# Fewer semaphore increments from TensorE, and scatters and gathers that no longer ask how far TensorE is

## The reference

```
agg = segment_sum(x[src], dst) / max(count, 1)                     # one matrix of edge counts serves all such sums
h   = relu(agg @ W1l.T + b1l + x @ W1r.T)                          # 256 -> 512
out = (segment_sum(h[src], dst) / count) @ W2l.T + b2l + h @ W2r.T # 512 -> 256
x   = layernorm(x + out)
# three hops:   H = segment_sum(H[src] * edge_weight, dst) @ Wn.T + H @ Ws.T + b   (elu between), x = layernorm(x + H)
# interaction:  messages (x @ W1)[src] + (x[src] * x[dst]) @ W2, scaled by degrees, summed by dst, then layernorm
# attention, 8 heads of 32, h = x @ W:
e   = leaky_relu(a_src[src] + a_dst[dst]);  m = segment_max(e, dst);  p = exp(e - m[dst])
out = segment_sum(h[src] * p, dst) / segment_sum(p, dst);  x = layernorm(x + layernorm(out + bias))
```

## Time and profile before

| | us |
|---|---|
| three runs | 2978.41, 2980.54, 2985.08 |
| median | 2980.54 |
| span of the profiled execution | 2974.2 |
| PE busy in the span | 2470.6 |
| DVE, ACT, POOL busy | 1396.0, 707.2, 936.7 |
| scatters L794 busy, 416 of them | 411.2 |
| gathers L2134 into `features_and_rows` busy, 376 of them | 401.7 |

### The profile page before, as it was taken

One profiled execution on the slowest core, in us unless ns is written; L12 is line 12 of the kernel. 1 busy time (PEld: TensorE's weight loads), 2 busy tenths in 40 slices (PEclk: granted clock), 3 DMA queues, 4 the chain that ended last, 5 costly groups with the idle time before them and its releaser, 6 DMA issues. The chain is left out here.

```text
span 2974.2 us, 32381 instructions
## 1 busy us (share of the span) xinstructions
PE 2470.6 (83%) x9483; PEld 1621.2 (55%) x9484; DVE 1396.0 (47%) x3940; ACT 707.2 (24%) x1552; POOL 936.7 (31%) x927
## 2 busy tenths in 40 slices
PE   3677789897987999999999999999977886457680
PEld 2444788343766555565556555577743444345560
DVE  7999656455665001030101001455575664546668
ACT  3776545111443000010001000255400000103112
POOL 0000256666666000000000000012167666576740
PEclk9888999998998999999999999999988998678885
DMA  6565678343344743444444434333558887646641
GB/s 233 243 253 225 212 238 264 118 138 97 112 121 137 152 151 129 151 134 151 129 152 133 151 119 145 93 106 102 113 168 271 278 282 245 209 132 190 192 127 43
DMA packets 209534, 493.89 MB, mean 166 GB/s; under 512 B 46457, under 2 KB 128430, under 8 KB 209134
## 3 DMA queue, kind: packets, MB, share of 16 engines
q1 hardware_dynamic: 135185, 301.30, 32.2%
q10 hardware_dynamic: 38173, 133.27, 12.8%
q0 software_dynamic: 36032, 57.60, 7.1%
HBM read 374.71 MB, written 117.32 MB: 165 GB/s over the span
## 5 line engine op out<-in xcount | busy, mean ns | idle before, releaser
L794 POOL DMA_INDIRECT table_dense_weights<-pair_weight,dst x416 | 411.2, 988 | 563.5 <-DVE weights_c L849 324.8
L1526 PE MATMUL banks<-own_term,features_and_rows 128*128 128x391 f32 (+1 forms) x1656 | 552.3, 491 | 0.0
L2134 POOL DMA_INDIRECT features_and_rows<-table_heads,src x376 | 401.7, 1068 | 191.4 <-issue 107.9
L1526 PEld LDWEIGHTS banks<-own_term,features_and_rows 128*128 128x128 f32 x1656 | 312.2, 189 | 226.8
L1552 DVE TENSOR_SCALAR features_and_rows<-banks,hop_bias 128x391 f32<-128x391 f32 (+1 forms) x24 | 15.0, 625 | 762.2 <-PE banks L1526 762.2
L954 PE MATMUL banks<-split_rows,count_columns 128*128 128x512 f32 x1200 | 322.1, 415 | 19.6 <-issue 12.6
L2531 PE MATMUL banks<-features_and_rows,edge_to_window 128*128 x880 | 233.4, 427 | 104.5 <-DVE edge_to_window L2492 71.6
L1526 PE MATMUL banks<-features_and_rows 128*128 128x391 f32 (+1 forms) x840 | 282.4, 491 | 0.0
L954 PEld LDWEIGHTS banks<-split_rows,count_columns 128*128 128x128 f32 x1200 | 226.3, 193 | 76.8 <-issue 21.7
L2531 PEld LDWEIGHTS banks<-features_and_rows,edge_to_window 128*128 128x128 f32 x880 | 181.3, 210 | 156.5 <-issue 122.5
L558 PE MATMUL banks<-features_and_rows,pair_and_bias_rows 128*128 128x400 f16 x806 | 184.3, 388 | 87.1 <-DVE features_and_rows L540 51.9
(11 more groups left out here) (425 smaller groups left out, 3016.8 us busy)
## 6 DMA issues: line engine op xcount, KB each, us to landing
hidden<-table_counts SPq DMA_DIRECT2D x305, 160.0 KB
table_dense_weights<-weights_c ACTq DMA_DIRECT2D x26, 1600.0 KB, 5.7
own_term<-table_dense_weights SPq DMA_DIRECT2D x52, 782.0 KB
features_and_rows<-table_rows_by_edge SPq DMA_DIRECT2D x58, 528.0 KB
own_term<-table_dense_weights SPq DMA_DIRECT2D x34, 780.5 KB
pair_and_bias_rows<-table_edge_rows ACTq DMA_DIRECT2D x50, 512.0 KB
weights_c<-table_edge_rows ACTq DMA_DIRECT2D x50, 512.0 KB
table_rows_by_edge<-features_and_rows SPq DMA_DIRECT2D x48, 528.0 KB
```

Source lines behind the costliest of these rows:

```text
L794: e.indirect_dma_start(out=self.table, out_offset=bass.IndirectOffsetOnAxis(ap=self.place[:, t:t + 1], axis=0), in_=self.values[:, t:t + 1 ...
L1526: m = e.matmul(psum[b][:, 0:wide], z_block(block)[:, f * P:(f + 1) * P], streamed[tile % STREAM][:, lo - from_column:lo - from_column + wi ...
L2134: e.indirect_dma_start(out=to[:, k, :], out_offset=None, in_=t_h, in_offset=bass.IndirectOffsetOnAxis(ap=src[:, t:t + 1], axis=0)).then_in ...
```

## The change

Four parts. (1) `T(..., last=False)` uses the new `pr.part`, which waits but raises nothing: in the transposes and dense layers only the last product of a group raises `done_pe`; `s_a_used` is raised in passes 1 and 2 at the groups 2 and 4 of five instead of at all; `s_mm` once in four steps; `s_picked` once in a cut of 16 stages, and the mask on DVE no longer waits for it. All numbers that others wait for are worked out anew (`used`, the merge's ends rounded up to a quad). (2) POOL's waits by PE's and DVE's progress go: `multiplied_beside` in the scatters, and `s_masked` in the gathers. Its waits for data (`done_dve`, DMAs landed, buffers free) stay. (3) Where a wait took its number from a register by `snap`, `wait_loaded` masks it with 511 into a second register. (4) One more DVE instruction rounds the merge's ends.

```diff
+    def part(self, e, fn, *waits):
+        def emit(eng):
+            for s, v in waits:
+                eng.wait_ge(s, v)
+            fn(eng)
+        self.queue[e].append(emit)
...
-        T = lambda fn, *w: pr.op("pe", fn, *w)
+        T = lambda fn, *w, last=True: pr.op("pe", fn, *w) if last else pr.part("pe", fn, *w)
+        def wait_loaded(e, sem, loaded, bound):
+            e.reg_alu(bound, loaded, 511, ALU.bitwise_and)
+            e.wait_ge(sem, bound)
...
-            def tiles(self, e, s, c, half_step=0):
-                for i, k in enumerate(range(c, UNROLL, 3) if s < THIRDS else range(c, UNROLL, 2)):
+            def tiles(self, e, s, c):
+                for k in range(c, UNROLL, 3) if s < THIRDS else range(c, UNROLL, 2):
                     t = s * UNROLL + k
-                    if i == 2:
-                        multiplied_beside(e, half_step, 1)
...
-        def multiplied_beside(e, half_step, half=0):
-            if IN_ROWS <= half_step < IN_LAYERS:
-                e.wait_ge(s_a_used, min(45 + 4 * (half_step - IN_ROWS) + 2 * half, of_group(Q1, 0) + NODE_TILES * COUNT_GROUPS - 1))
-            elif IN_LAYERS <= half_step < IN_SECOND:
-                e.wait_ge(pr.done["pe"], dense_layers_from[0] + max(1, 6 * (half_step - IN_LAYERS) - 10 + 3 * half))
-            elif IN_SECOND <= half_step < IN_TURNS:
-                e.wait_ge(s_a_used, min(of_group(Q2, 0) + 4 * (half_step - IN_SECOND) + 2 * half, of_group(Q3, 0) - 1))
...
+        USED_AT = (COUNT_GROUPS // 2, COUNT_GROUPS - 1)
+        used = lambda q, g: q * len(USED_AT) + (1 if g <= USED_AT[0] else 2) if q < Q3 else of_group(q - Q3, g) + Q3 * len(USED_AT)
...
-                    e.wait_ge(s_a_used, of_group(q - 1, g))
+                    e.wait_ge(s_a_used, used(q - 1, g))
...
-                m.then_inc(s_a_used, 1)
+                if g in USED_AT:
+                    m.then_inc(s_a_used, 1)
...
-                          freed if q == 0 else None, scaled[c], xt_ready if q == 0 else None, l_w)
+                          freed if q == 0 else None, scaled[c], xt_ready if q == 0 else None, l_w, last=q == len(pairs) - 1)
...
-                          freed if mt == 0 else None, made[c])
+                          freed if mt == 0 else None, made[c], last=mt == K_HID - 1)
...
-                if k % 2 == 0 and stage + k // 2 > 0:
-                    e.wait_ge(s_masked, stage + k // 2)
...
-                e.matmul(psum[2 + b % 2][:, 0:n], sum_heads[head_rows, at:at + P], masked[i % 2][head_rows, 0:n],
-                         start=(r == 0), stop=(r == SCAN_ROWS - 1)).then_inc(s_picked, 1)
+                if r == SCAN_ROWS - 1:
+                    m.then_inc(s_picked, 1)
...
-                if i >= 2:
-                    e.wait_ge(s_picked, i - 1)
...
-                e.wait_ge(s_mm, quad * GROUP + (mm0 - GROUP))
+                e.wait_ge(s_mm, quad + (mm0 - 1))
...
-                             start=False, stop=False, skip_group_check=True).then_inc(s_mm, 1)
+                    if k % GROUP == GROUP - 1:
+                        m.then_inc(s_mm, 1)
```

More of the change, by code:

```diff
@@ L142, in op @@
         return sem, self.count[sem.name]
+    def part(self, e, fn, *waits):
+        waits = [w for w in waits if w is not None]
+        def emit(eng):
[3 more added lines that the diff above has]
+        self.queue[e].append(emit)
     def dma(self, e, sem, out, in_, *waits):
@@ L547, in build_pe @@
             pe_regs.extend(e.alloc_register(f"step_{k}") for k in range(2 * REGS_AT_ONCE))
-            regs = pe_regs
+            regs, bound = pe_regs, e.alloc_register("zeroed_windows")
             for s in range(BUILD_STEPS):
@@ L555, in build_pe @@
                 e.wait_ge(s_step_hot, s + 1)
-                e.wait_ge(s_zeroed, e.snap(regs[2 * n + 1], min_val=3, max_val=WINDOWS + 2))
+                wait_loaded(e, s_zeroed, regs[2 * n + 1], bound)
                 for q in range(2):
@@ L565, in build_act @@
             regs = [e.alloc_register(f"window_end_{k}") for k in range(ROTATING)]
+            bound = e.alloc_register("window_end_step")
             for b in [RUN_BANK, RUN_BANK + 1, *range(ROTATING)]:
@@ L810, in step @@
             def step(self, e, s):
-                multiplied_beside(e, 2 * s)
-                self.tiles(e, s, 0, 2 * s)
+                self.tiles(e, s, 0)
                 if s > 1:
@@ L815, in step @@
                 if s:
[L816 to L817 removed]
+                    self.rest(e, s - 1)
             def end(self, e):
@@ L1009, in run @@
                 m = multiply_rows(e, psum[0], lambda k: count_columns[:, k, :], (k,), 0, True)
-                if k % COUNT_GROUP == COUNT_GROUP - 1:
+                if k % COUNT_GROUP == COUNT_GROUP - 1 and k // COUNT_GROUP in USED_AT:
                     m.then_inc(s_a_used, 1)
@@ L1035, in residual_gnn @@
                 next(steps)
-        multiplied_tail = (s_a_used, of_group(Q1, COUNT_GROUPS - 1))
+        multiplied_tail = (s_a_used, used(Q1, COUNT_GROUPS - 1))
         tail_split = split(K_FOLD, psum[0][:, 0:DIM], multiplied_tail)
@@ L1167, in running_sum @@
             before = lambda n: ps[:, n * 32:n * 32 + NODE_TILES]
-            T(lambda e: e.matmul(before(0), triangle, counts, start=True, stop=True), freed, tri)
+            T(lambda e: e.matmul(before(0), triangle, counts, start=True, stop=True), freed, tri, last=False)
             m = T(lambda e: e.matmul(before(1), ones[:, :], counts, start=True, stop=True))
@@ L1220, in from_hidden @@
                                               split_of[j], xb)
-        dense_layers_from[0] = pr.count[pr.done["pe"].name]
         to_hidden(0)
@@ L1268, in residual_gnn @@
         widen(Q2 + 1)
-        split(K_FOLD, psum[0][:, 0:DIM], (s_a_used, of_group(Q2, COUNT_GROUPS - 1)))
+        split(K_FOLD, psum[0][:, 0:DIM], (s_a_used, used(Q2, COUNT_GROUPS - 1)))
         folded2 = [build_fold(1, s_row2)]
@@ L1309, in residual_gnn @@
         V(lambda e: e.reciprocal(rdeg[:, :], rdeg[:, :]), d2)
-        turned_from[0] = pr.count[pr.done["pe"].name]
         in_groups(turn0)
@@ L1762, in residual_gnn @@
                 m = T(lambda e, ps=ps, j=j, k=k: e.transpose(ps[:, k * P:(k + 1) * P], xT[:, k, j * P:(j + 1) * P], ident[:, :]),
-                      freed, *hops_done)
+                      freed, *hops_done, last=k == K_IN - 1)
             turned_late[j] = i, ps, m
@@ L2061, in first_rows @@
             e.wait_ge(*prepared["index"])
-            e.wait_ge(s_a_used, of_group(Q3 + NODE_TILES - 1, COUNT_GROUPS - 1))
+            e.wait_ge(s_a_used, used(Q3 + NODE_TILES - 1, COUNT_GROUPS - 1))
             for k in range(ROWS_KEPT // 2):
@@ L2127, in residual_gnn, with gather_group @@
         FIRST = [0, 1, 2, *range(6, PLACES), 3, 4, 5]
-        def gather_group(e, quad, to, sem, stage=0):
+        def gather_group(e, quad, to, sem):
             for k in range(GROUP):
                 t = quad * GROUP + k
-                if k % 2 == 0 and stage + k // 2 > 0:
-                    e.wait_ge(s_masked, stage + k // 2)
                 e.indirect_dma_start(out=to[:, k, :], out_offset=None, in_=t_h,
@@ L2138, in place_free @@
             if quad >= PLACES:
-                e.wait_ge(s_mm, mm0 + (quad - PLACES) * GROUP + GROUP - 1 + NODE_TILES)
+                e.wait_ge(s_mm, mm0 + (quad - PLACES) + (GROUP - 1 + NODE_TILES) // GROUP)
             elif quad < IN_CHAIN:
@@ L2339, in dve @@
                 bent = bent_cut(lo, n)
-                e.wait_ge(s_picked, SCAN_ROWS * (b + 1))
+                e.wait_ge(s_picked, b + 1)
                 e.wait_ge(s_held, 2 * b + 2)
@@ L2537, in merge_act @@
             ends_of_node = [e.alloc_register(f"node_end{k}") for k in range(NODE_TILES)]
+            bound = e.alloc_register("node_end_step")
             e.load(ends_of_node, merge_control[0:1, MERGE_STEPS:MERGE_STEPS + NODE_TILES])
```

51 lines of the change are left out of this document (24 added, 27 removed).

## The result

The changed kernel takes 3371.6 us (median of 5 runs, 3363.7 to 3416.8) where the kernel before takes 2980.5 (5 runs): a ratio of 1.1298, with a 95% interval of 1.1273 to 1.1324. Its profiled execution was the longest of the five, with a span of 3415.0 us; two later profiles of the same kernel have 3360.3 and 3363.6, and of the 51 to 55 us between them 48 to 51 lie in the scan.

A forecast was written before the change was run, and what follows sets the result against it. PE was taken as the engine nearest to the bound, held up by increments late beside POOL's indirect DMAs. Scan −40, merge −25, passes and dense layers −15 made −80 from 2974.2, 2894 profiled; forecast 2900, range 2820 to 3000.

The forecast's parts named there:

- the slower rival: Passes, dense layers and scan: without pauses PE's increments are always late, however few; 3105 us, chance 0.20.
- 106 + 37 + 29 = 172: Holes seen before: scan 106 us over its even stages, PE's "issue" in passes and dense layers 37.5, POOL's merge waits 28.9.
- If late increments stand in a line, a line half or a quarter as long is served sooner: PE's increments in passes, dense layers, scan and merge: raising fewer makes late ones visible sooner; basis of the −80 us.
- the last rival: Whole kernel: increments were never the cause, late ones come as before; time within 0.2%, 6 us; chance 0.05.
- So this part pays for nothing on the path itself: Gathers without the condition: no gain of their own, but without this the scan's −40 us would stop near −10.
- took 13 us off for it: Scan: half the lateness would give −53 us; because POOL no longer pauses, −40 was taken.
- before 900: Passes and dense layers: a sign that the forecast holds, scatters over before 900 us in the changed profile.
- +26: Slower rival, dense layers: 53 groups at 4.6 us an increment take 241 us instead of 215.
- +29: Slower rival, scan: 4.9 us a stage until its gathers end near 2510, then 2.16 us.
- +69: Slower rival, pass 2: a tile takes 18 us instead of 7.4 until scatters end at about 887.
- 3 us per increment: Slower rival: lateness from about which it decides; there scan and merge still gain what the passes lose.
- −25 forecast: Merge: increments in quads free most of POOL's 28.9 us idle for PE's steps; bounds 0 and −29.

The follow-up runs named there:

- scatters_left_out: The changed kernel without its 416 scatters, so the hops multiply by a table of zeros; 2799.7 us, ratio 0.9988, on the chip without lateness.
- fewer_increments_only: The changed kernel with both kinds of POOL's conditions on progress put back; 2975.7 against 2971.5 us for the kernel before, ratio 1.0005.

## Why the prediction was wrong

The forecast was 2900 us and a gain; the slower rival had 0.20 and 3105 us, the range ended at 3000.

**The reading of the trace was right in its first half.** PE's work becomes visible microseconds late, only beside POOL's indirect DMAs, and the best evidence is the chip on which none of 1541 is late in any profile and the kernel before takes 2803 us instead of 2980. The difference is 178 us, and I had looked for 106 + 37 + 29 = 172 in scan, passes and merge. That the sums meet is luck. `scatters_left_out`, which takes 2800 us there, begins its hops 101 us earlier than the kernel before does on the other chip (scatters are 6 of these). It gains 77 us in the scan, loses 34 between scan and merge, where the merge waits for POOL's gathers, and gains 33 in the merge. So the passes and dense layers held more than twice what I read from them, and the scan less: its 112 stages take 264 us even without lateness, not 242.

**"If late increments stand in a line, a line half or a quarter as long is served sooner" was the step that failed.** `fewer_increments_only` tried it alone: −80 us forecast, a ratio of 1.0005 (0.9988 to 1.0023) measured. That is what the last rival, with its 0.05, said of this part. A line of increments is not what the trace has. PE's weight loads and products, most of them without an increment, start 0.7 to 3.5 us apart in the same stretches, so what is thinned is a small part of what is held back. I could have seen it: "issue" at L1197, L954 and L1080 in the earlier trace rows is PE waiting for nothing, and I put it down to ACT and DVE being late.

**"So this part pays for nothing on the path itself" was wrong by its sign.** I had noted that long waits end near POOL's pauses and took 13 us off for it. The conditions are the pauses: without them +220 us in passes and dense layers, +162 in the scan. POOL did not even finish its scatters sooner: the last ends at 997 us after 977, where I had named "before 900" as a sign, since POOL then waited for the values that DVE makes (L848, 64.0 and 47.7 us).

**The slower rival was the true one, and its price was too low.** It named the side of the mechanism (POOL without pauses makes PE's increments late) and gave +124 us. Pass 1 wasn't in its sum (+153 measured). The dense layers were put at +26 (+118) and the scan at +29 (+163 and +165 in the profiles of ordinary length), from 4.6 us an increment; there a mask of the scan waits up to 21.0 us. The +29 doesn't follow from its own numbers either: 323 us of gathers at 4.9 us a stage are 66 stages, the 46 left at 2.16 us are 99 us, and 422 us in all are 74 more than the window of 348. With that the rival stood at 3150 us. Pass 2 was put at +69 and won 45, since scatters ended in pass 1 and the dense layers, which had become that much longer, and the transposes and pass 2 ran with POOL silent. Its point of decision, 3 us per increment, hung on increments as the unit.

**Expected by the last rival alone:** that the merge wouldn't move (−25 forecast, 335 and 337 us measured). POOL's waits for PE in it are 22.2 us after 28.9. From the first of the 25 lookups to the last gather it takes 279 us (3032 to 3311) after 281 (2591 to 2872). The merge had no conditions on progress to lose, and a quarter of the increments gave it nothing.

What was right: the masks cost nothing (1.0004), nor does the rounding instruction, which is in `fewer_increments_only` (1.0005), and an increment costs PE nothing in a busy stretch. By the Trainium skill ("TensorE: Matmul & The Clock Gate", The cost: per-tile semaphore tail) 850 fewer increments would have been an estimated 22 us on PE's path; the ratio of `fewer_increments_only`, 1.0005 ± 0.0018, is 1.5 us with 5 either way, so this kernel shows no such tail.

**What is shown and what stays open.** Shown, in four sessions on chips with lateness: neither the number of increments nor POOL's knowledge of PE makes the loss; what makes it is how densely POOL issues. On these chips an issue every 1.61 us holds nothing back, every 1.43 us it does where counts are loaded and not in the dense layers, every 1.35 us all over. With denser issues it depends on how many stand in a row: 4 with 1.2 us more between do little harm, 8 some, 16 much. That fits a store of POOL's writes that fills when issues are denser than it empties and behind which PE stands: at three places of the changed kernel's trace the held increments came 2.7 us after the last of 12 issues in a row, 4.8 us after the last of 32, 7.8 us after the last of 58, 0.1 us more for each issue. Other places scatter (one run of 32 has 1.4 us). This picture is argued, not shown; it put the limit at 1.39 us, and 1.43 was not enough. What of PE passes there, why DVE is held in the dense layers and not in the scan, why in steps of 0.7 us, and why one chip is free of it, stays open. That the changed kernel would equal the one before on that chip is likely (`scatters_left_out` runs its scan there in 264 us) but wasn't met in a run.

## What to carry to other kernels

A wait that seems to serve no data may be there for its pause: before taking it out, look at what ends the long waits elsewhere, and try it alone. If TensorE shows "issue" between products that wait for nothing, and others wait for "remote", while GpSimd issues indirect DMAs, space those out before thinning semaphores (here groups of four issues, with four fills of 1.0 us in all between them, were 2.4% faster than the conditions on progress). And compare kernels on one chip only: between two chips the same kernel differed by 6%, nearly half of what this change cost.

## What the runs showed of the hardware that was not expected

- One chip ran the kernel before in 2803 us; in five sessions on others its medians were 2972 to 2988. The first has no lateness: 0 of 1541 increments are late in the kernels profiled on it, beside 521 of 2117 in the kernel before on another. That lateness is all of the difference is not shown.
- Beside indirect DMAs every 1.27 us, TensorE's products of 0.37 us started 2.1 to 3.5 us apart, and increments came up to 46 us late. Of DVE's 66 of 2476 were late, by up to 8.9 us, 65 of them in the dense layers. ACT's came within 0.1 us but for one.
- Late increments of TensorE between 400 and 880 us: none of 177 with 1.61 us between issues, 54 of 104 with 1.43 us, 60 of 94 with 1.35 us.
- A fill of 128x128 on GpSimd takes 0.23 us, and behind an indirect DMA adds only 0.1 us to the interval, since the gap before the next issue falls from 0.30 to 0.17 us.
